# One small product and a broadcast load for the mixing's bias, in a fused conditioned mixing and ternary feed-forward kernel

## What is computed

```python
h = gelu(cond @ W0 + b0); h = gelu(h @ W1 + b1)
att = softmax(h @ W2 + b2)                       # (64 batches, 8)
agg_w = einsum('bk,koi->boi', att, weight)       # per-batch mixing matrix
agg_b = att @ bias_k                             # (64, 64): per-batch bias, one value per output row
y = einsum('boi,bih->boh', agg_w, x) + agg_b[:, :, None]
out = x + bitlinear(bitlinear(y, w_gate) * bitlinear(y, w_up), w_down)   # weights rounded to -1, 0, 1
```

## Time and profile before

| | us |
|---|---|
| median of 3 runs | 1807.35 (1807.18 to 1808.13) |
| the profiled execution, its own time | 1806.68 |
| its span in the profile | 1804.9 |

### The profile page before, as it was taken

One profiled execution on the slowest core, in us unless ns is written; L12 is line 12 of the kernel. 1 busy time (PEld: TensorE's weight loads), 2 busy tenths in 40 slices (PEclk: granted clock), 3 DMA queues, 4 the chain that ended last, 5 costly groups with the idle time before them and its releaser, 6 DMA issues.

```text
span 1804.9 us, 29867 instructions
## 1 busy us (share of the span) xinstructions
PE 1743.9 (97%) x11911; PEld 1164.9 (65%) x11911; DVE 1130.8 (63%) x1839; ACT 541.4 (30%) x844; POOL 150.9 (8%) x104
## 2 busy tenths in 40 slices
PE   5698899999999999999999999999999999999999
PEld 3344454444545969678685868669695877768584
DVE  6989965686442555856467555855468455766364
ACT  4668441122211313323132312323032322333030
POOL 0864510110000000000000000000000000000000
PEclk9799999999999999999999999999999999999999
DMA  8437511243002212242113312241022412222021
GB/s 306 164 124 258 148 47 71 100 179 123 1 24 78 105 41 103 79 148 83 62 62 135 115 41 93 72 166 62 22 102 103 145 62 93 72 98 83 21 103 47
DMA packets 55325, 177.98 MB, mean 99 GB/s; under 512 B 5904, under 2 KB 6224, under 8 KB 55184
## 3 DMA queue, kind: packets, MB, share of 16 engines
q1 hardware_dynamic: 52704, 161.77, 25.7%
q0 software_dynamic: 2480, 14.22, 2.0%
HBM read 144.97 MB, written 31.00 MB: 97 GB/s over the span
## 4 chain that ended last, share of the span: by engine, by line
PE 91%; DVE 3%; issue 2%; ACT 2%; POOL 1%; DMA 0%; SPq 0%; DVEq 0%; ACTq 0%; POOLq 0%
PE ps L795 43%; PE ps L607 26%; PE ps L852 20%; PE ps L813 2%; DVE msk L1302 1%; ACT g_r L977 1%; PE ps L689 1%; POOL ys L574 1%; ACT wgT L1006 0%; DVE aT L247 0%; DVE msk L1294 0%; DVE prod L1330 0%; POOL ab L585 0%; DVE ys L1221 0%; DMA inter<-in_L_cond_b_dram 0%
## 5 line engine op out<-in xcount | busy, mean ns | idle before, releaser
L795 PE MATMUL ps<-yp,wgT 128*128 128x256 f16 x3528 | 773.7, 273 | 1.8 <-DVE xr L1351 1.0
L795 PE MATMUL ps<-wuT,wgT 128*128 128x256 f16 x3528 | 773.7, 273 | 0.0
L795 PEld LDWEIGHTS ps<-yp,wgT 128*128 128x128 fp8e4 x3528 | 345.3, 98 | 48.4 <-issue 7.5
L795 PEld LDWEIGHTS ps<-wuT,wgT 128*128 128x128 fp8e4 x3528 | 345.2, 98 | 41.4
L852 PE MATMUL ps<-wdT,inter 128*128 128x512 fp8e4 x1680 | 371.3, 379 | 0.0
L852 PEld LDWEIGHTS ps<-wdT,inter 128*128 128x128 f16 x1680 | 163.9, 98 | 194.6 <-issue 1.1
L1616 DVE SCALAR_TENSOR_TENSOR xr<-ps,osc,xr 128x512 f32<-128x512 f32 x180 | 134.1, 748 | 146.6 <-PE ps L852 111.5
L1565 DVE TENSOR_TENSOR wdT<-ps,msk 128x512 f32<-128x512 f32 (+1 forms) x66 | 44.0, 667 | 179.1 <-PE ps L795 179.1
L607 PE MATMUL ps<-yp,wgT 128*128 128x512 f16 x672 | 153.3, 387 | 2.9 <-DVE yp L1256 1.8
L607 PE MATMUL ps<-yp,wuT 128*128 128x512 f16 x672 | 150.0, 379 | 0.0
L607 PE MATMUL ps<-wdT,inter 128*128 128x512 fp8e4 x672 | 147.7, 379 | 0.0
(11 more groups left out here) (231 smaller groups left out, 1737.3 us busy)
## 6 DMA issues: line engine op xcount, KB each, us to landing
wgT<-wcomb SPq DMA_DIRECT2D x60, 896.0 KB, 4.7
wdT<-dcomb SPq DMA_DIRECT2D x12, 2240.0 KB, 10.1
xa<-in_x_dram SPq DMA_DIRECT2D x8, 2048.0 KB, 7.8
out_dram<-xr SPq DMA_DIRECT2D x64, 256.0 KB, 2.0
wdT<-in_L_ffn_w_up_dram SPq DMA_DIRECT2D x10, 512.0 KB, 4.1
wcomb<-raw POOLq DMA_DIRECT2D x11, 448.0 KB, 2.8
ys<-in_L_ffn_w_down_dram SPq DMA_DIRECT2D x9, 512.0 KB, 4.6
wcomb<-msk POOLq DMA_DIRECT2D x10, 448.0 KB, 2.8
```

Source lines behind the costliest of these rows:

```text
L795: last = nc.tensor.matmul(out, w, operand(i, OPERAND[what])[:, k, :], start=(start and h + k + i == 0), stop=(k == KQ - 1 and i == 1), ski ...
```

## The change

The bias of all 64 batches is made once, in the start: one product of `attT` and `biask` (64 x 64 result) into `ps[6]`, copied by ScalarE to `biasb`, and stored by ScalarE's own queue to a scratch `biasd` in DRAM. Each chunk's 8 x 64 values are 2 KB in one run there, and one transfer loads them into all 128 partitions of `bbc`. For chunk 0 ScalarE's queue issues that load, behind a wait for the store; for the others SP issues it right behind `load_x(c+1)`, with a wait for the last use of `scl` (or, for chunk 1, for the last quantisation). `bprod`, the eight `agg_b` of TensorE and of VectorE and GpSimd's product are gone, and GpSimd's step for the next chunk starts one wait earlier.

```diff
+        def bias_row(c):
+            return biasd[bass.ds(c * BC, BC), :].rearrange("b o -> (b o)").unsqueeze(0).broadcast_to([P, TOK])
 # SP
+            def load_bias(c):
+                sp.dma_start(bbc[:, :], bias_row(c)).then_inc(s_bias, 16)
             load_x(1)
+            sp.wait_ge(s_q, NQ)
+            load_bias(1)
             store(0)
             def next_x(c):
                 sp.wait_ge(s_xr, NT * c + NT)
                 sp.wait_ge(s_y, KH * c + KH)
                 load_x(c + 1)
+                sp.wait_ge(s_ysc, KH * c + SCD)
+                load_bias(c + 1)
 # GpSimd
-                nc.gpsimd.tensor_tensor(bprod..., attT..., biask..., ALU.mult).then_inc(s_bprod, 1)
-            pool.wait_ge(s_cv, 8)
-            pool.wait_ge(s_cond3, 48)
-            next_chunk(0)
                 pool.wait_ge(s_y, KH * c + KH)
-                pool.wait_ge(s_bb, c + 1)
                 next_chunk(c + 1)
 # TensorE
+            pe.wait_ge(s_cond3, 48)
+            pe.wait_ge(s_cv, 8)
+            mm(ps[6][0:B, 0:C], attT[:, :], biask[:, :]).then_inc(s_bb, 1)
             pe.wait_ge(s_cv, 11)
-            def agg_b(c):
-                pe.wait_ge(s_bprod, c + 1)
-                if not (isinstance(c, int) and c == 0):
-                    pe.wait_ge(s_p2v, c)
-                mm(YB[1][:, :], ones[0:NK, :], bprod[:, :]).then_inc(s_bb, 1)
             def conv(c, k):
-                if k == 1:
-                    pe.wait_ge(s_bbv, c + 1)
+                if k == 0 and isinstance(c, int) and c == 0:
+                    pe.wait_ge(s_bbv, 1)
+                if k == 1 and not (isinstance(c, int) and c == 0):
+                    pe.wait_ge(s_p2v, c)
 # ScalarE
-            for n in (2, 3):
-                raw_sum(n)
+            raw_sum(2)
+            act.wait_ge(s_bb, 1)
+            nc.scalar.copy(biasb[:, :], ps[6][0:B, 0:C]).then_inc(s_bbv, 1)
+            raw_sum(3)
+            act.wait_ge(s_bbv, 1)
+            nc.scalar.dma_start(biasd, biasb[:, :]).then_inc(s_bst, 16)
+            act.wait_ge(s_bst, 16)
+            nc.scalar.dma_start(bbc[:, :], bias_row(0)).then_inc(s_bias, 16)
 # VectorE
-            def agg_b(c):
-                dve.wait_ge(s_bb, c + 1)
-                V.tensor_copy(bbc[:, :], YB[1][:, :]).then_inc(s_bbv, 1)
             def conv(c, k):
                 if k == 0:
-                    dve.wait_ge(s_bbv, c + 1)
+                    dve.wait_ge(s_bias, 16 * (c + 1))
```

More of the change, by code:

```diff
@@ L166, in adaln_ternary_ffn @@
         ablk = sb("ablk", [P, NT, P], f32)
-        bprod = sb("bprod", [NK, TOK], f32)
+        biasb = sb("biasb", [B, C], f32)
         bbc = sb("bbc", [P, TOK], f32)
@@ L261, in adaln_ternary_ffn @@
         dcomb = nc.dram_tensor("dcomb", [NPR, P, PART // 4], f32).ap()
+        biasd = nc.dram_tensor("biasd", [B, C], f32).ap()
         wd_flat = wdT[:, :, :].rearrange("p a n -> p (a n)")
@@ L360, in adaln_ternary_ffn @@
         s_ablk = sem("s_ablk")
-        s_bprod = sem("s_bprod")
         s_bb = sem("s_bb")
         s_bbv = sem("s_bbv")
+        s_bst = sem("s_bst")
+        s_bias = sem("s_bias")
         s_y = sem("s_y")
@@ L555, in next_chunk @@
             def next_chunk(c):
[L557 to L562, removed]
                 for h in range(2):
-                    pool.wait_ge(s_bprod if h == 0 else s_ablk, c + 1 if h == 0 else 2 * c + 1)
-                    pool.sem_inc(s_turn_pool, 1)
+                    if h:
+                        pool.wait_ge(s_ablk, 2 * c + 1)
+                        pool.sem_inc(s_turn_pool, 1)
                     block_diagonal(nc.gpsimd, c, h)
-            pool.wait_ge(s_cv, 8)
-            pool.wait_ge(s_cond3, 48)
-            next_chunk(0)
             pool.wait_ge(s_scl, 1)
@@ L623, in _ @@
             nc.tensor.transpose(ps[5][:, 0:B], attr, ident[0:B, 0:B]).then_inc(s_pe, 1)
+            pe.wait_ge(s_cond3, 48)
+            pe.wait_ge(s_cv, 8)
+            mm(ps[6][0:B, 0:C], attT[:, :], biask[:, :]).then_inc(s_bb, 1)
             pe.wait_ge(s_cv, 11)
-            pe.wait_ge(s_cond3, 48)
             def agg_w(h, g):
@@ L867, in downs @@
                         norms_T(c + 1)
-            agg_b(0)
             for k in range(KH):
@@ L890, in _ @@
                     group(0, FT + n)
-                    if n == UP - 3:
-                        agg_b(1)
             for k in range(KH):
@@ L899, in chunk @@
                     group(c, j)
-                    if more and j == UP + 9:
-                        agg_b(c + 1)
                     if more and j - UP - 11 in range(KH):
@@ L915, in pairs @@
                         product(c, p - 1, "P4")
-                    if more and p == 1:
-                        agg_b(c + 1)
                     if more and p - 2 in range(KH):
@@ L1392, in _ @@
                 if what == "U":
-                    if n == UP - 2:
-                        agg_b(1)
                     product(0, n)
@@ L1501, in chunk @@
                         split(c, u - 1)
-                    if more and u == 11:
-                        agg_b(c + 1)
                     if more and u - 12 in range(KH):
```

## The result

The changed kernel takes 1797.76 us, median of 5 runs (1796.91 to 1798.84), against 1807.35 us for the kernel before on the same chip (5 runs, 1806.96 to 1808.15). The ratio is 0.9948 with a 95% interval of [0.9938, 0.9958]: 9.6 us faster. In microseconds the interval is a gain of 7.6 to 11.2. The forecast was 1799.4 us with a range of 1798.0 to 1803.0.

The account below looks back on a forecast made before the run. TensorE's stream, 91% of the span, was taken as the bound. Seven products at 1.14 us gave 8.0 us off, all else nothing: 1807.35 - 8.0 = 1799.4 us, range 1798.0 to 1803.0.

Parts of the forecast that it names:

- a product costs 1.14 us of stream: TensorE's stream: each agg_b removed between its neighbours takes 1.14 us off the chain, kept in full.
- seven of eight count: agg_b(1) to agg_b(7) come off TensorE's chain, agg_b(0) in the start does not: 8.0 us off.
- the odd 12.33: The 12.33 us TensorE piece behind agg_b: removal might save 0.1 us more there, used for the range's lower end.
- eight copies of VectorE and eight products of GpSimd ... I count nothing: Removing this work was priced at nothing, as both engines wait for TensorE or are done long before.
- wrong for (a): Sign in the profile: an addition of the bias released by a transfer in chunk 1 or at the start.
- 2.3 to 3.3 us: Start: slack of the first bias load, there at 25.4 and needed at 27.69, at the latest 28.65; cost nothing.
- the 0.8 us of the broadcast load: Every chunk: the bias load lands 0.8 us after load_x, its rows spreading over the engines as load_x's do.
- (a): Rival: bias somewhat late in chunk 1 or the start, 1 to 4 us given back, 1800.4 to 1803.4; chance 0.12.
- (b): Rival: TensorE's freed time comes back as waits for ScalarE and VectorE, 1803.4 if half, 1807 if all; chance 0.05.
- (c): Rival, start: store and first load queue behind SP's loads, bias 16 us late, 1815 us; chance 0.05.
- (d): Rival: the bias load's 128 rows all on one DMA engine, 10 us each, total 1829 us; chance 0.02.
- The estimate by its section "Anatomy of one DMA — SWDGE (gpsimd) path": Start: about 2.0 us fixed plus bytes at 436 GB/s, store and load 4.6 us together, bbc there at about 21.

Follow-up runs that it names:

- keep_pe: The changed kernel with seven unread TensorE products put back at the old places of agg_b(1) to agg_b(7): 1805.38 us, ratio 0.9993.
- before_again: The kernel before, unaltered, measured and traced a second time: 1807.53 us, ratio 1.0.
- after_again: The changed kernel, unaltered, measured and traced a second time on another chip: 1797.00 us against 1806.97, ratio 0.9942.
- keep_both: The changed kernel with all eight GpSimd and all eight TensorE products put back unread, VectorE's copies left out: 1807.26 us, ratio 0.9998.
- pool4: The changed kernel with GpSimd's eight products put back unread, the one for chunk 1 made four times in a row: 1803.64 us, ratio 0.9977.
- awake2: The changed kernel with 56 unread TensorE products ahead of the first mixing and 170 more in three later waits of the start: 1805.49 us, ratio 0.9987.

## Why the prediction came out as it did

**Right: what bounds, and TensorE's term.** The steps "a product costs 1.14 us of stream" and "seven of eight count" hold: 1.15 us where the pieces join, 1.11 to 1.34 us per chunk, and about 8 us for putting the seven back (keep_pe). By the traces the term is 8.3 us, 0.3 more than the 8.0 of the sum. The lower bound, that the odd 12.33 might hide 0.1 us more, was hardly needed: the join saved 1.15, not 1.25. Over the four looped chunks the mean period fell from 206.57 to 205.35 us, 1.22 rather than 1.15. The 0.07 stands at the loop top or is scatter (before_again and after_again have 206.47 and 205.27). The seven products are taken off together in every run, so what a single one is worth is read from the traces alone.

**Wrong: "eight copies of VectorE and eight products of GpSimd ... I count nothing".** The reason given was that both engines wait for TensorE or have been done long before, read from the shares of the whole span. For the copies that holds (keep_both). It does not hold for GpSimd's product in the quantisation stretch of chunk 0, where VectorE is on the chain and TensorE waits for it. There the product didn't need to be on the chain itself: it slowed the engine that was. It was worth 0.8 us. The trace of the kernel before would have told it. The same form of mask, a pair of 128x512 from line 1294, takes 2.02 us at 229.47, and 0.71 us where it starts just after GpSimd has ended (VectorE, then GpSimd, kernel before):

```profile
213.79 0.71 DVE L1294 TENSOR_SCALAR msk<-xr,thr 128x512 fp8e4<-128x512 f32 x2
...
211.70 2.04 POOL L585 TENSOR_SCALAR ab<-xr,thr 128x704 bf16<-128x704 f32 x1 [1.94 <-DVE msk L1302]
```

Of that stretch only the earlier trace rows stood in my working, and GpSimd's records were not among them. The changed kernel still pays some of it: the end of GpSimd's 2.04 us operation from 228.33 and its first copy into ablk at 230.32 run beside the pair at 229.65, and it takes 1.38 us, not 0.71. The size of the hold is 0.7 to 0.8 us of VectorE's time for each 1.2 us product of GpSimd (pool4). The Trainium skill has a rule that bears on it, "SBUF — State Buffer", section "SBUF: two separate sides": VectorE and GpSimd share a pair of ports, and where an instruction of VectorE uses it (in some of its modes, or with two inputs from SBUF against a GpSimd instruction that reads SBUF), whichever starts first takes the pair for the whole instruction and the other is blocked. The traces agree in kind: VectorE's instructions last longer just where GpSimd works. They differ in size, for 0.7 to 0.8 us is less than the whole 1.2 us. No run here shows the ports themselves.

With it the sum would have been 8.0 + 0.8 = 8.8, and with TensorE's term as the traces have it 8.3 + 0.8 = 9.1. The 8.9 us between the two profiled spans are near both by luck: that pair holds 0.2 us of loss in the start, and the other pair is 12.2 us apart. The medians say 9.6 and 10.0, and the first interval, 7.6 to 11.2 us, contains 8.0, 8.8 and 9.1 alike: that 8.0 was too small is shown by the traces, not by the medians. The rest, 0.5 to 0.9 us over 9.1, is not accounted for by any record. Part may be the start: there the attd products had a product of GpSimd beside them too, took 2.00 us and take 1.29 now. In the pair of traces shown that gain is lost again, and the changed kernel is 0.34 us behind at 175 us; in after_again the way to the first threshold is 1.4 us shorter than in before_again. The clock scatters by more than what is looked for. Whether the start gained anything stays open.

**The start: right in kind, off in size.** The forecast for ScalarE's store was 4 us from issue to landing, and it was 5.9 us. For the load it was 4.8 us, and it was 6.7 us. Forecast, bbc was there at 25.4; it was there at about 27.2, and the first addition was released by the transfer, which is what "wrong for (a)" was to look like:

```profile
27.28 0.69 DVE L1216 TENSOR_TENSOR ys<-ps,bbc 128x512 f32<-128x512 f32 x1 [2.40 <-DMA bbc<-biasd]
28.77 0.69 DVE L1216 TENSOR_TENSOR ys<-ps,bbc 128x512 f32<-128x512 f32 x1 [0.79 <-PE ps L609]
```

It cost nothing here, and the margin of the prediction says why: the second addition waits for TensorE again, at 28.77, and it did not move before the first started after 28.1. The slack was not 2.3 to 3.3 us but about 0.8. In after_again it was nothing for the second addition, which follows the first without a gap (both stand in one row, 1.33 us from 27.38); only the third, which waits 1.34 us for TensorE, kept the late bias from costing time. The cover also shrank from the other side: TensorE is busy with the first mixing for the whole of 25 to 26 us in the changed kernel, where it was busy for 0.35 us of it before (the window shown above).

**Chunk 1: right in kind, and tighter than forecast.** The forecast was 252.4 (at most 252.6) against a need at 254.0. The chain of the changed kernel shows the load in it (start us, us, what):

```profile
243.20 0.38 SPq L444
...
243.62 9.03 DMA bbc<-biasd
252.65 0.04 DVEq L1215
...
252.75 0.68 DVE inter L1337
253.43 0.61 DVE ys L1216
```

It landed at 252.65, 0.25 us later than forecast; VectorE made one product of the other stream at 252.75, and the addition stands at 253.43 on the chain (its row starts at 253.35), against 255.12 before. The slack is 0.7 us, not 1.4. The hold that went away is not the reason: it brought the need forward by 0.6 us, and the issue of load_x(1) with it, from 243.82 to 243.20. The mis-sized term is the 0.8 us of the broadcast load. It landed 9.45 us after load_x was issued, where 7.8 + 0.8 = 8.6 were forecast: load_x took 8.0 us, and the bias came about 1.4 us behind it. The chain names the load as the last to come, and it is the next thing that binds if this stretch is made faster.

**The rivals.** (a), a late bias with 1 to 4 us lost: the two places came within 0.7 and 0.8 us of it (in after_again the start came closer still) and lost nothing. (b), freed time that comes back as waits: not seen, the piece of 26.36 us has no gap. (c), store and load behind SyncE's backlog, 14.1 us each: not seen. The 5.9 and 6.7 us were measured while all transfers together moved 411 GB/s on average, and most of SyncE's tiles of 512 KB that were issued then landed after 13.1 to 15.9 us (medians of the groups xr, raw, wuT and inter), so ScalarE's transfers passed most of that backlog. The Trainium skill, "DMA: Bandwidth & Descriptors", section "Queues, rings and completion order", says that each DMA engine takes turns between the queues that have work, packet by packet, and the trace agrees. The estimate by its section "Anatomy of one DMA — SWDGE (gpsimd) path" was 4.6 us for the two together. That section's figures are a fit for transfers that GpSimd issues, which these are not; the trace has 12.6 us, at full load. (d), a load on one engine with 10 us: not seen, the load took 8.0 us (median) with load_x in front of it, and VectorE never waited for it in a looped chunk.

## What to carry to other kernels

An engine that is idle most of the time and off the chain can still cost: look at what runs beside it where the chain is on another engine, and compare the same instruction with and without it. Here that was GpSimd beside VectorE, and it cost 0.7 to 0.8 us for each 1.2 us. A product that stands inside an unbroken stream of TensorE is worth the distance between its neighbours' starts less one neighbour, times the number of chunks, and that estimate (1.14 us) held within 0.1 us on average. Two traces of the same kernels can differ by more than the effect looked for: lay them side by side position by position, and see where the difference arises before it is believed.

## What was not expected of the hardware

- A product of GpSimd over only 8 partitions (8x512, f32, 1.20 us) lengthened VectorE's masks over 128 partitions by 0.8 us: 3.41 us instead of 2.61 us. The attd products in the start took 2.00 us instead of 1.29 us.
- A short idle stretch of TensorE can cost more than itself. In pool4 a hold that was 2.0 us longer was followed by a granted clock of 0.50 to 0.55 (1.2 GHz), and 16 products took 6.14 us instead of 3.57.
- Filling TensorE's idle stretch with 56 unread products kept its clock at the upper level (2.4 GHz): the first mixing took 2.02 us instead of 3.75 us.
- The moment at which the clock falls and comes back in the start differs between executions of one kernel by a microsecond or more. A gain of half a microsecond there can't be read from one trace each.
- A loop can lose 2.27 us at its top to a stall that no wait explains, in a kernel that differs only ahead of the loop (awake2).
